# Channel attention on one Trainium2 core: the norms of queries and keys from a product on VectorE and a sum over the rows by TensorE

## The reference

```python
xt = x.reshape(b, c, n).transpose(0, 2, 1)     # x: after the group norm
q, k, v = jnp.split(xt @ w_qkv, 3, axis=-1)    # each to heads of d = 24 channels
q = q / jnp.maximum(jnp.sqrt(jnp.sum(q * q, axis=-2, keepdims=True)), EPS)
k = k / jnp.maximum(jnp.sqrt(jnp.sum(k * k, axis=-1, keepdims=True)), EPS)
k = k * temperature
attn = jax.nn.softmax(jnp.einsum('bhpn,bhnq->bhpq', k, q), axis=-1)
out = jnp.einsum('bhnp,bhpq->bhnq', v, attn)   # back to (b, n, c)
out = out @ w_out + b_out                      # and x + out
```

## Time and profile before

| | |
|---|---|
| median of three runs | 373.96 us (373.68 to 374.70) |
| the profiled execution | 374.76 us |
| its span, first to last instruction | 372.8 us |
| mean granted TensorE clock | 0.980 of full |
| TensorE busy | 331.2 us, 89% |
| VectorE busy | 283.2 us, 76% |
| ScalarE busy | 235.9 us, 63% |
| GpSimd busy | 150.4 us, 40% |

### The profile page before, as it was taken

How to read it: one execution, slowest core, us unless ns; L and a number is a source line. 1 busy time by engine, 2 the same in 40 slices (tenths; PEclk the granted TensorE clock), 3 DMA queues, 4 the chain that set the end, 5 groups by cost and what they waited for, 6 DMA issues and landing times.

```text
span 372.8 us, 9327 instructions
## 1 busy us (share of the span) xinstructions
PE 331.2 (89%) x3724; PEld 233.4 (63%) x3724; DVE 283.2 (76%) x666; ACT 235.9 (63%) x410; POOL 150.4 (40%) x133
## 2 busy tenths in 40 slices
PE   0048856999999999999999999999999999999795
PEld 0036645875778566865777577856686577765452
DVE  4889855887699669986799769966998665359774
ACT  1098489763997299747996399729974699610200
POOL 0079858301970169203950197016920395001000
PEclk9999976899999999999999999999999999999999
DMA  7999900004994279815991499427981563034766
GB/s 235 359 286 246 244 16 3 2 2 139 300 323 132 86 233 326 247 44 137 336 335 44 134 297 338 124 87 226 320 261 45 165 217 88 2 105 150 230 213 192
DMA packets 30826, 67.73 MB, mean 182 GB/s; under 512 B 5504, under 2 KB 12096, under 8 KB 30784
## 3 DMA queue, kind: packets, MB, share of 16 engines
q1 hardware_dynamic: 30544, 66.56, 56.7%
q10 hardware_dynamic: 240, 0.59, 0.6%
HBM read 29.38 MB, written 28.31 MB: 155 GB/s over the span
## 4 chain that ended last, share of the span: by engine, by line
PE 64%; ACT 15%; issue 10%; DVE 5%; DMA 2%; SPq 2%; POOL 1%; ACTq 0%; POOLq 0%
PE u_ps L927 30%; PE g_ps L927 17%; PE s_ps L927 10%; ACT h_sb L543 4%; ACT tok L581 4%; ACT xn L537 3%; PE u_ps L976 2%; DMA wo<-in_L_conv_w_out_dram 2%; PE u_ps L977 2%; ACT h_sb L550 1%; DVE x_sb L855 1%; PE u_ps L979 1%; PE u_ps L978 1%; SPq L354 1%; SPq L359 1%
## 5 line engine op out<-in xcount | busy, mean ns | idle before, releaser
L474 POOL TENSOR_TENSOR l_sb<-xn,h_sb 128x768 f16<-128x768 f32 x63 | 103.8, 1649 | 56.0 <-ACT h_sb L543 55.7
L855 DVE SCALAR_TENSOR_TENSOR x_sb<-u_ps,bias,x_sb 128x384 f32<-128x384 f32 x144 | 85.9, 613 | 24.2 <-PE u_ps L927 24.1
L927 PE MATMUL g_ps<-tok 128*128 128x64 f16 (+1 forms) x864 | 87.1, 241 | 3.4 <-ACT tok L581 2.9
L537 ACT ACTIVATE xn<-x_sb,rb 128x768 f32<-128x768 f32 x63 | 63.6, 1020 | 29.7 <-POOL rb L486 29.7
L581 ACT COPY tok<-u_ps 128x384 f32<-128x384 f32 x144 | 65.0, 485 | 19.8 <-PE u_ps L979 18.6
L927 PEld LDWEIGHTS g_ps<-tok 128*128 128x128 f16 x864 | 57.0, 99 | 28.5 <-ACT tok L581 5.8
L728 DVE BATCH_NORM_STATS2 bnst<-x_sb 128x6 f32<-128x384 f32 x144 | 69.9, 543 | 5.3 <-DMA x_sb<-in_x_dram 5.2
L927 PE MATMUL u_ps<-h_sb,ml 128*128 128x384 f16 (+1 forms) x336 | 73.2, 327 | 0.0
L543 ACT ACTIVATE h_sb<-x_sb,rb 128x768 f16<-128x768 f32 x63 | 64.4, 1022 | 0.0
L976 PE MATMUL u_ps<-id,h_sb 128*128 128x128 f16 x288 | 48.9, 223 | 8.2 <-DVE l_sb L718 7.4
L977 PE MATMUL u_ps<-id,l_sb 128*128 128x128 f16 x288 | 48.9, 223 | 0.0
(11 more groups left out here) (144 smaller groups left out, 567.6 us busy)
## 6 DMA issues: line engine op xcount, KB each, us to landing
x_sb<-in_x_dram SPq DMA_DIRECT2D x48, 384.0 KB, 5.4
out_dram<-x_sb SPq DMA_DIRECT2D x48, 384.0 KB, 2.9
out_dram<-x_sb SPq DMA_DIRECT2D x48, 192.0 KB, 2.8
x_sb<-in_x_dram SPq DMA_DIRECT2D x45, 192.0 KB, 5.4
hl<-h_sb SPq DMA_DIRECT2D x48, 96.0 KB, 2.8
hl<-l_sb SPq DMA_DIRECT2D x48, 96.0 KB, 3.0
x_sb<-in_x_dram ACTq DMA_DIRECT2D x3, 192.0 KB, 4.2
w<-in_L_conv_w_qkv_dram SPq DMA_DIRECT2D x1, 288.0 KB, 7.4
```

What stands on the lines that cost most here:

```text
L474: nc.gpsimd.tensor_tensor(l_sb[:, par, t, cols], xn[:, c % XN_RING, :], h_sb[:, par, t, cols], ALU.subtract).then_inc(l_ok, 1)
L537: nc.scalar.activation(xn[:, c % XN_RING, :], xcol(q, t, g * GW, GW), ACT.Identity, bias=rb[:, par, 1, t:t + 1], scale=rb[:, par, 0, t:t + ...
L855: V.scalar_tensor_tensor(out=xs, in0=block_ps(n), scalar=bias[:, t:t + 1], in1=xs, op0=ALU.add, op1=ALU.add).then_inc(out_ok, 1)
L927: return nc.tensor.matmul(dst, lhs, rhs, start=start, stop=stop, skip_group_check=True)
```

## The change

The norms are no longer taken from diagonals of products. VectorE multiplies T, as it stands in PSUM, by the weights in SBUF, element by element (`pw`, behind each `low_t`); ScalarE copies that to fp16 (`high_products`), VectorE subtracts this copy for the low half (`low_products`), and TensorE sums over the rows with `pw16` as weights and two columns of ones and zeros, one for each image (`squares`). VectorE clamps the eight sums (`norms`). `scores` keeps only the products of queries with keys, and the halves of T only the query columns. The lists move too.

```diff
-PE_B = {0: ["gram"], 2: ["sums"], 4: ["w0"], 6: ["w1"], 12: ["scores"]}
+PE_B = {0: ["gram"], 2: ["sums"], 4: ["w0"], 6: ["w1"], 10: ["scores"], 13: ["squares"]}
...
-POOL_B = ["power", 0, 1, 2, 3, 4, "norms", 5, 6, 7, 8]
+POOL_B = ["power", 0, 1, 2, "norms", 3, 4, 5, 6, 7, 8]
...
-                nc.scalar.copy(tq[:, k, 0, :], src[:, 0:2 * C]).then_inc(th_ok, 1)
...
+                nc.scalar.copy(tq[:, k, 0, :], src[:, 0:C]).then_inc(th_ok, 1)
+
+            def high_products(q):
+
+                need(act, n_mm, q)
+                for k in range(3):
+                    act.wait_ge(pw_ok, 3 * q + k + 1)
+                    nc.scalar.copy(pw16[:, k, 0, :], pw[:, k, :]).then_inc(ph_ok, 1)
...
-                dve.wait_ge(s_mm, q + 1)
-                one = id32[0:HC, 0:HC].unsqueeze(1).unsqueeze(1).to_broadcast([HC, 2, 2, HC])
-                ch = Chain(dve, diag, q * DIAG, DIAG)
-                V.tensor_tensor(dg[:, 4:8, :].rearrange("p (b j) c -> p b j c", b=2), qk_ps[:, :, :, 0, :], one, ALU.mult)
-                ch.then(V.tensor_tensor(dg[:, 0:4, :].rearrange("p (b j) c -> p b j c", b=2), kk_ps, one, ALU.mult))
-                ch.then(V.tensor_reduce(n8[:, :], dg[:, :, :], AX_X, ALU.add))
-                ch.then(V.tensor_scalar(n8[:, :], n8[:, :], NORM_EPS ** 2 * NORM_FACTOR, None, ALU.max))
...
+                dve.wait_ge(n_mm, q + 1)
+                V.tensor_scalar(n8[:, :], n_ps, NORM_EPS ** 2 * NORM_FACTOR, None, ALU.max).then_inc(diag, 1)
...
-                V.tensor_tensor(tq[:, k, 1, :], src[:, 0:2 * C], tq[:, k, 0, :], ALU.subtract).then_inc(tl_ok, 1)
+                V.tensor_tensor(tq[:, k, 1, :], src[:, 0:C], tq[:, k, 0, :], ALU.subtract).then_inc(tl_ok, 1)
+                if k == 0:
+
+                    need(dve, pl_ok, 3 * q)
+                V.scalar_tensor_tensor(out=pw[:, k, :], in0=src[:, 0:2 * C], scalar=W_SCALE, in1=(w1 if k == 2 else w0)[:, 0:2 * C],
+                                       op0=ALU.mult, op1=ALU.mult).then_inc(pw_ok, 1)
+
+            def low_products(q):
+                for k in range(3):
+
+                    dve.wait_ge(ph_ok, 3 * q + k + 1)
+                    V.tensor_tensor(pw16[:, k, 1, :], pw[:, k, :], pw16[:, k, 0, :], ALU.subtract).then_inc(pl_ok, 1)
...
+            def squares(q):
+
+                pe.wait_ge(pl_ok, 3 * q + 3)
+                for a in range(4):
+                    c = C - C * (a // 2) + HC * (a % 2)
+                    terms = [(pw16[:, k, i, c:c + HC], side[:, k, :]) for k in range(3) for i in (0, 1)]
+                    dst = n_ps.rearrange("p (s b j) -> p s j b", s=2, b=2)[:, a // 2, a % 2, :]
+                    for k, (lhs, one) in enumerate(terms):
+                        last = mm(dst, lhs, one, k == 0, k == len(terms) - 1)
+                last.then_inc(n_mm, 1)
```

More of the change, by code:

```diff
@@ L91 @@
 LAST_PE_A = {0: ["m"]}
-LAST_PE_B = {0: ["gram"], 2: ["w0"], 3: ["w1"], 5: ["scores"], 10: ["flip"], 16: ["v"]}
+LAST_PE_B = {0: ["gram"], 2: ["w0"], 3: ["w1"], 6: ["scores"], 7: ["squares"], 10: ["flip"], 16: ["v"]}
 LAST_ACT_A = {0: ["m"]}
-LAST_ACT_B = ["t0", "t1", "t2", "exp", "v"]
+LAST_ACT_B = ["t0", "t1", "t2", "p", "exp", "v"]
 LAST_POOL_B = ["norms"]
 LAST_VEC_A = {0: ["m0", "m1"]}
-LAST_VEC_B = {0: ["gram"], 2: ["z"], 3: ["t0", "t1", "t2"], 5: ["norms"], 8: ["spread"], 10: ["soft_in"], 12: ["soft_out"],
-              15: ["v"]}
+LAST_VEC_B = {0: ["gram"], 2: ["z"], 3: ["t0", "t1", "t2"], 5: ["lo"], 7: ["norms"], 9: ["spread"], 10: ["soft_in"], 12: ["soft_out"], 15: ["v"]}
 SUMS_AT = next(n for n, what in PE_B.items() if "sums" in what)
@@ L180, in preact_attention @@
         z16 = sb("z16", [P, 2, C], F16)
-        tq = sb("tq", [P, 3, 2, 2 * C], F16)
-        dg = sb("dg", [HC, 8, HC])
+        tq = sb("tq", [P, 3, 2, C], F16)
+        pw = sb("pw", [P, 3, 2 * C])
+        pw16 = sb("pw16", [P, 3, 2, 2 * C], F16)
+        side = sb("side", [P, 3, 2], F16)
         n8 = sb("n8", [HC, 8])
@@ L270, in preact_attention @@
         r8_ok = sem("r8_ok")
+        pw_ok = sem("pw_ok")
+        ph_ok = sem("ph_ok")
+        pl_ok = sem("pl_ok")
+        n_mm = sem("n_mm")
         diag = sem("diag")
@@ L287, in preact_attention @@
         out_ok = sem("out_ok")
[L289 removed]
+        STAT, GVAR, NORM, SOFT, ATTN = 6, 4, 2, 5, 6
         def high_count(k):
@@ L673, in _ @@
             V.memset(wl1[C1:P, :], 0.0)
+            ones = ((0, slice(0, P), 0), (1, slice(0, P), 1), (2, slice(0, C1), 0), (2, slice(C1, P), 1))
+            for k, rows, b in ones:
+                V.memset(side[rows, k, b:b + 1], 1.0)
+                V.memset(side[rows, k, 1 - b:2 - b], 0.0)
             for z in (wmh, wml):
@@ L1072, in scores @@
                         kc = slice(C + HC * j, C + HC * j + HC)
[L1073 to L1082 removed]
+                        terms = [(tq[:, b, 0, qc], wh0[:, kc]), (tq[:, b, 1, qc], wh0[:, kc]), (tq[:, b, 0, qc], wl0[:, kc]),
+                                 (tq[:, 2, 0, qc], wmh[:, b, kc]), (tq[:, 2, 1, qc], wmh[:, b, kc]),
+                                 (tq[:, 2, 0, qc], wml[:, b, kc])]
+                        for k, (lhs, w) in enumerate(terms):
+                            last = mm(qk_ps[:, b, j, :], lhs, w, k == 0, k == 5)
+                last.then_inc(s_mm, 1)
+            def squares(q):
[7 more added lines that the diff above has]
+                last.then_inc(n_mm, 1)
             def flip(q):
@@ L1166, in _ @@
             small_steps = {"gram": finish_gram, "w0": lambda q: gram_weights(q, False),
-                           "w1": lambda q: gram_weights(q, True), "scores": scores, "flip": flip,
+                           "w1": lambda q: gram_weights(q, True), "scores": scores, "squares": squares, "flip": flip,
                            "v": attn_values, "m": folded_weights}
```

35 lines of the change are left out of this document (14 added, 21 removed).

## The result

The changed kernel takes 386.60 us (median of 4 runs, 386.09 to 388.03) against 373.82 (373.66 to 374.70, 4 runs) of the kernel before on the same chip: ratio 1.0352, 95% interval 1.0324 to 1.0381. It is slower by 3.5%. Its profiled execution took 386.85 us; span 385.1, mean granted clock 0.963 (0.980 before).

The account below looks back on a forecast made before the run. TensorE is busy 89%, but the once-per-pair handover to ScalarE's token copy decides. First stage +1.8, pairs +10.2, tail -1.0, clock +4.4 sum to +15.4 us: 389.4 against the median; range 377 to 399.

Parts of the forecast that it names:

- scores, squares on TensorE, up to the next result: TensorE, per pair: 24 score matmuls of 96 columns take 1.07 us, the 24 added squares 1.0 us.
- first transposes earlier against the copies of T: TensorE, per pair: saves 1.0 us (3.06 - 1.07 - 1.0) ahead of the token copy, but off the path.
- token copy later with the power early: GpSimd's power ahead of low parts 3 and 4 delays ScalarE's chunk 7 and token copy: 1.7 us per full pair.
- later by ScalarE's copies alone: ScalarE's path grows 1.26 us per pair by three fp16 copies; alone, the token copy starts 0.7 us later.
- the six pairs without falls: Six full pairs, each with the token copy 1.7 us later: 10.2 us.
- start up to the first value matmuls: First stage: ScalarE's copies, and low part 4 behind the power, make the token copy some 1.8 us later.
- clock falls: TensorE's gap before the gram grows to 2.7 us; two falls of the granted clock at 2.2 us, 4.4 us in all.
- tail: Last pair: the sums for the norms come 1.0 to 1.2 us earlier and the whole tail follows; taken as 1.0 us.
- The 62 ns: TensorE: floor between matmul starts where the sequencer decodes in software; squares would take 1.5 us, norms 0.5 us later.
- The wait of 0.13 us for the third product: ScalarE: its third fp16 copy waits for VectorE's third product, 0.13 us per pair.
- a race open by under 0.1 us: VectorE's third low-half subtraction against GpSimd's next low part at 217.2: costs 0 or some 1.7 us; 0 taken.
- the rival: Third low half loses to GpSimd in full pairs: 2.45 us per pair, four falls, +24.3 us, 398; chance 0.2.

Follow-up runs that it names:

- run 1: The changed kernel with GpSimd's power for the norms put back behind five low parts: 376.54 us, ratio 1.0083 to the kernel before.
- run 7: The kernel before without its 24 key-by-key products on TensorE, norms of the keys left out: 371.29 us, ratio 0.9965.
- Run 3: The kernel before with three 128x384 fp16 copies added on ScalarE into a buffer that nothing reads: 379.66 us, ratio 1.0176.
- run 2: The kernel before with only GpSimd's power moved to where the change puts it: 407.14 us, ratio 1.0893.
- Run 4: The changed kernel with ScalarE's three fp16 copies replaced by a second product on VectorE: 402.67 us, ratio 1.0765 to the kernel before.
- run 5: The changed kernel with the product kept in PSUM, VectorE writing both halves, ScalarE's copies gone, power behind five low parts: 377.36 us, ratio 1.0123.
- Run 9: The changed kernel with 13 useless matmuls of 384 columns in TensorE's gap ahead of the gram: 383.29 us, ratio 1.0228 to the kernel before.
- run 6: As run 5 without the fp32 product and its low half, so 12 squares and less exact norms: 371.74 us, ratio 0.9957.

## Why the prediction was right

The time forecast was 389.4, measured 386.6; the mechanism is the one forecast. Against the profiled executions the sum was +15.4, measured +12.1. Over the span it was 3.1 us too high: 2.1 at the start, 1.2 in the clock and 0.4 in the tail, less 0.7 in the pairs.

| Step of the prediction | forecast | measured |
|---|---|---|
| scores, squares on TensorE, up to the next result | 1.07, 1.0 us | 1.21, 1.07 |
| first transposes earlier against the copies of T | 1.0 | 0.67 |
| token copy later with the power early | 1.7 | 1.84 |
| later by ScalarE's copies alone | 0.7 | 0.52 (run 1) |
| the six pairs without falls | +10.2 | +10.9 |
| start up to the first value matmuls | +1.8 | -0.3 |
| clock falls | 2 x 2.2 = +4.4 | 3, together +3.2 |
| tail | -1.0 | -1.4 |

**TensorE.** Squares took 0.045 us each like the scores with the same 96 weights. Its saving was set too high: the transposes start 12.46 us behind the copies of T instead of 13.13. Multiplying 24 by 0.045 left out the 0.13 us between scores and results, which are in the 3.06 that it was taken from. The 62 ns of the Trainium skill (TensorE: Matmul & The Clock Gate, section "Wait — 56ns, not 53.3ns?") would have made the squares 1.5 us, an estimate; these rows don't agree with it. That the saving at the token copy is off the path is right: TensorE waits there for 2.38 us, and even in the kernel before 1.08 us less were worth 0.33 (run 7). TensorE's time up to the squares is on the path, through the clamp and the power.

**ScalarE.** The term was 1.26 us and came out near 1.1: the last two `xn` of stage B start 12.35 us behind the copy of T in run 1 and 11.27 in the earlier trace rows. The wait of 0.13 us for the third product did not occur (1.32 us for three without a wait). Run 1 shows the term by itself: 0.52 us per pair against 0.7. Run 3 shows it less cleanly, since there a clamp of 1.45 us makes TensorE late as well.

**The power.** This step carries the result, and runs 1 and 2 show it both ways: taken out of the change it gives 10 us back; put into the kernel before it costs nearly 34. The change makes the sums early enough that the early power costs 10 and not 34; it would have been better not to move it. The prediction had GpSimd ready for the power 0.1 us behind the clamp; it was ready 0.67 us before it could start, so the clamp, and TensorE's squares ahead of it, end last there.

**Low halves and GpSimd.** I took 0 for a race open by under 0.1 us. It came out so, but by little: the third subtraction started at 224.25 and GpSimd's low part at 224.37, and it ran 0.55 us. That it held was luck as much as working. Run 4 shows the rival's mechanism: once the halves stand later by VectorE's extra products, one takes 2.00 us. So a running instruction of GpSimd holds such a subtraction up: it starts at 234.60 within a low part that ends at 236.19, and ends at 236.60. The Trainium skill (SBUF — State Buffer, section "Who interferes with whom") states this; the 2.00 us agree. In run 4 the token copy came 3.15 us later than in the earlier trace rows (16.81 against 13.66 behind the copy of T), where the rival had 2.45; by run 5 VectorE's three more products are some 0.2 us of that.

**The clock.** The step that was off. Run 9 shows that the falls in the full pairs hang on what TensorE does in the gap. The length of the gap alone does not decide: the same 2.4 us stand ahead of the gram of every full pair, and only every second has a fall. I had priced a fall by the first stage, 2.2 us, where the low clock lasted from 61.2 to 68.1 us, 6.0 of it behind the gram; here it lasts 3.4 us and costs about 1.06. For each us at the low clock the two agree, 0.36 and 0.31; it was the length that I had wrong. Three falls came, not two, and that count was a guess. The two errors partly cancel.

**The start.** The sum had +1.8 for the handover of the first stage. From the copies of T to the gram it did grow, by 13.24 - 11.74 = 1.5. But gram to value matmuls took 9.39 instead of 10.35 us, since the granted clock rose again sooner after that gram (66.7 instead of 68.1, with the gram at 62.7 instead of 62.1), and the copies of T came 0.84 earlier. They stand between 48.9 and 51.6 us over the kernels run here; what moves them I could not attribute.

## What to carry to other kernels

Look at the engine that the chain passes to once per stage and at its slack there: 1.08 us taken from the busiest engine was worth 0.33, while 1.3 us given to an engine with 0.46 us of slack cost 0.9. Compare durations too, and not only waits: in both of these runs a clamp grew from 0.20 to 1.3 or 1.45 us, because it had come to stand beside another GpSimd instruction. A small instruction in an in-order queue has the price of what waits behind it; move it only if its input is early by more than the work it overtakes, and try the change with and without that move. When TensorE is idle ahead of a dense stretch, look at the granted clock behind it: filling the gap with useless wide matmuls bought back 3.3 us.

## What the runs showed of the hardware that I had not expected

- Thirteen matmuls of 384 columns in the gap kept the clock at 1.00; 36 of 24 columns, leaving 1.51 us idle, did not. Gaps of 1.1 to 1.3 us (runs 1 and 6) were followed by no fall in the full pairs. Which of gap and work decides was not separated.
- Falls came in every second pair at a gap of 2.4 us, and in every full pair in run 4, with gaps of some 3.1 us (21.8 us over seven waits) and pairs of 44.54 us.
- In run 2, with gaps of 3.64 us, every full pair has a fall too, and two of the six last 6.8 us (steps of 46.4 us; 45.1 with 3.4).
- A clamp of 96x8 in fp32 from SBUF to SBUF takes 0.20 us in the kernel before, where it starts 0.2 us ahead of the end of GpSimd's low part, and 1.45 and 1.28 us in runs 3 and 7, where it starts near a low part's start; in all three runs it ends 0.02 to 0.03 us behind it. The changed kernel's clamp reads PSUM and takes 0.16 us, in run 1 in the middle of a low part.
- A matmul with fp32 weights of 96 columns and two fp32 columns beside it is two instructions of 0.09 us each.
